# Scatters and gathers ordered by pick in a sparse expert layer: tiles wait for the level of their expert, gathers for the last expert of their pick

## The reference

```python
logits = jnp.einsum('bsh,eh->bse', x, router_w) + expert_bias
scores = jax.nn.softmax(logits, axis=-1)
top_w, top_idx = jax.lax.top_k(scores, TOP_K)          # TOP_K = 4
top_w = top_w / jnp.sum(top_w, axis=-1, keepdims=True)
g = jnp.einsum('bsh,khe->bske', x, gate_proj)          # 16 x (256, 224)
u = jnp.einsum('bsh,khe->bske', x, up_proj)
act = jax.nn.silu(g) * u
out = jnp.einsum('bske,keh->bskh', act, down_proj)     # 16 x (224, 256)
sel = jnp.take_along_axis(out, top_idx[..., None], axis=2)
return jnp.sum(sel * top_w[..., None], axis=2)
```

## Time and profile before

| | us |
|---|---|
| median of three runs (lowest, highest) | 670.77 (670.66, 671.4) |
| the profiled execution | 671.04 |
| its span in the trace | 669.1 |
| first scatter issued | 106.14 |
| first expert tile's load issued | 149.01 |
| first gather issued, last gather issued | 262.28, 301.69 |
| PE busy in the span | 545.4 (82%) |

### The profile page before, as it was taken

One profiled execution on the slowest core, in us unless ns is written; L12 is line 12 of the kernel. 1 busy time (PEld: TensorE's weight loads), 2 busy tenths in 40 slices (PEclk: granted clock), 3 DMA queues, 4 the chain that ended last, 5 costly groups with the idle time before them and its releaser, 6 DMA issues.

```text
span 669.1 us, 10928 instructions
## 1 busy us (share of the span) xinstructions
PE 545.4 (82%) x3365; PEld 470.0 (70%) x3365; DVE 372.1 (56%) x989; ACT 228.5 (34%) x583; POOL 267.5 (40%) x247
## 2 busy tenths in 40 slices
PE   7898966009999999305987796699999999999994
PEld 4665655008998988203653374599999999999994
DVE  4665685703444444563999865866444444444445
ACT  4653432203555554213501033123333233323334
POOL 4473025751678962770378600310431404314000
PEclk9996897557999999655999877789999999999998
DMA  8999301622667764430000030020202102000001
GB/s 251 383 387 382 122 1 64 219 93 73 200 194 227 215 207 131 142 106 21 0 1 0 18 124 1 0 72 1 72 1 72 42 30 71 0 0 0 0 0 63
DMA packets 54571, 66.71 MB, mean 100 GB/s; under 512 B 5745, under 2 KB 49538, under 8 KB 54530
## 3 DMA queue, kind: packets, MB, share of 16 engines
q10 hardware_dynamic: 31872, 31.07, 13.7%
q1 hardware_dynamic: 19298, 26.18, 12.5%
q0 software_dynamic: 3360, 8.93, 4.3%
HBM read 36.02 MB, written 30.15 MB: 99 GB/s over the span
## 4 chain that ended last, share of the span: by engine, by line
PE 61%; DVE 11%; POOL 9%; issue 5%; DMA 4%; ACT 2%; ACTq 0%; POOLq 0%; DVEq 0%
PE PS L1646 45%; POOL FA L671 4%; POOL xg L636 4%; PE PS L1914 3%; DMA FA<-xg 3%; DVE FA L1600 2%; DVE PS L1582 2%; PE PS L1939 1%; PE PS L1743 1%; PE PS L1721 1%; PE PS L2034 1%; PE PS L1963 1%; PE PS L2046 1%; PE PS L1706 1%; DVE EQ L1369 1%
## 5 line engine op out<-in xcount | busy, mean ns | idle before, releaser
L1646 PE MATMUL PS<-EW,XH 128*128 128x384 f32 (+2 forms) x732 | 208.7, 367 | 6.0 <-DVE SQ L1398 4.4
L1646 PEld LDWEIGHTS PS<-EW,XH 128*128 128x128 f32 x732 | 126.5, 193 | 10.5 <-DVE SQ L1398 4.7
L1398 DVE SCALAR_TENSOR_TENSOR SQ<-SIL,CW,PS 128x96 f32<-128x96 f32 x256 | 69.1, 311 | 115.7 <-ACT SIL L846 114.8
L1646 PE MATMUL PS<-EW,XL 128*128 128x384 f32 (+2 forms) x366 | 129.4, 353 | 0.0
L1646 PE MATMUL PS<-EW,EHH 128*128 128x256 f32 (+1 forms) x476 | 101.8, 289 | 0.2
L846 ACT ACTIVATE SIL<-PS 128x192 f32<-128x192 f32 x128 | 42.5, 332 | 160.8 <-PE PS L1646 160.8
L1646 PE MATMUL PS<-EW,EHL 128*128 128x256 f32 (+1 forms) x286 | 80.2, 281 | 0.0
L1646 PEld LDWEIGHTS PS<-EW,EHH 128*128 128x128 f32 (+1 forms) x476 | 78.0, 188 | 1.2 <-issue 0.5
L602 POOL TENSOR_TENSOR round_mark<-round_mark 128x1 f32<-128x1 f32 x10 | 2.2, 217 | 181.0 <-PE PS L1646 132.0
L1646 PEld LDWEIGHTS PS<-EW,XL 128*128 128x128 f32 x366 | 70.2, 192 | 2.1
L1646 PEld LDWEIGHTS PS<-EW,EHL 128*128 128x128 f32 (+1 forms) x286 | 53.8, 188 | 0.0
(11 more groups left out here) (348 smaller groups left out, 1058.0 us busy)
## 6 DMA issues: line engine op xcount, KB each, us to landing
xg<-EQ ACTq DMA_DIRECT2D x1, 16384.0 KB, 61.5
EG<-in_gateup SPq DMA_DIRECT2D x16, 448.0 KB, 4.1
FA<-xg ACTq DMA_DIRECT2D x47, 128.0 KB, 2.5
yg<-FA ACTq DMA_DIRECT2D x47, 128.0 KB, 2.2
ED<-in_down SPq DMA_DIRECT2D x16, 224.0 KB, 4.5
EG<-in_gateup SPq DMA_DIRECT2D x4, 768.0 KB, 4.6
FA<-in_gateup SPq DMA_DIRECT2D x4, 768.0 KB, 4.7
yg<-EQ ACTq DMA_DIRECT2D x1, 1920.0 KB, 8.6
```

What stands on the lines that cost most here:

```text
L1398: ins = dve.scalar_tensor_tensor(out=HH[:, pos % 2, h:h + W], in0=SIL[:, s, j * W:(j + 1) * W], scalar=c, in1=bank(s)[:, I + j * W:I + (j ...
L1646: ins = pe.matmul(o, l, r, start=start and i == 0, stop=stop and i == n - 1, skip_group_check=True)
```

## The change

1. The picks of a token are sorted by expert number, smallest first: DVE negates the four indices and takes MAX8 of them per token tile. So pick 0 can be of experts 0 to 12, pick 1 of 1 to 13, pick 2 of 2 to 14, pick 3 of 3 to 15. The softmax over the picks is now taken over all 16 logits, and the picks' weights are selected from that inside the tile loop.
2. The scatters go by pick. First 14 of the first half's 16 (picks 0 to 2, then pick 3 of tiles 0 and 1), then the second half's by pick, with the first half's last two among them. When all eight of a pick have landed POOL raises `level` by one (`landed`).
3. A tile's load waits for the level of its expert (expert 0: level 1; 1: 2; 2: 3; others: 4), read from a table for each of the first 12 tiles. Before, the first load waited for all 32 scatters.
4. The gathers go by pick. All tiles' pick 0 when the stores up to pick 0's last expert have landed, then pick 1 likewise, then picks 2 and 3 by tile when all are stored. PE adds 8 small matmuls that count the picks by expert (`picked_experts`), for the last expert of each pick. With this case's inputs these are experts 10, 12 and 15, so 30, 34 and 40 tiles. The marks are made three times. An eighth `BACK` buffer lies in `OGATE`.
5. `pack_slots`, the weights and the store counts are cut in seven parts that DVE does inside the tile loop, after iterations 8, 10, 12 (weights), 14, 16, 18 (rows) and 20 (counts).
6. All 47 tiles of `yg` are zeroed, and that transfer moves forward into the first attention (unit 28 of its 40).

```diff
+            for k in range(TOP0 - 1):
+                for t in range(HALF):
+                    scatter(t, k)
+            for t in range(HALF // 2):
+                scatter(t, TOP0 - 1)
+            pool.wait_ge(slots_ready, 2)
+            pool.wait_ge(x_act, NT)
+            for k in range(TOP0 - 1):
+                for t in range(HALF, NT):
+                    scatter(t, k)
+                    if k > 0 and t == HALF + 1:
+                        landed(k - 1)
+            for t in range(HALF // 2, NT):
+                scatter(t, TOP0 - 1)
+                if t == HALF // 2 + 1:
+                    landed(TOP0 - 2)
+            landed(TOP0 - 1)
+            pool.wait_ge(level, TOP0)
...
+            for k in range(2):
+                stored_up_to(k, k)
+                for t in range(NT):
+                    gather(t, k)
+            stored_up_to(TOP0 - 1, 2)
             for t in range(NT):
...
+                for k in range(2, TOP0):
+                    gather(t, k)
...
+                if u == YG_ZERO_AT:
+                    act.dma_start(yg.rearrange("(n p) d -> p n d", p=P),
...
+                if i < EARLY_TILES:
+                    act.wait_ge(level, act.value_load(tile_level[0:1, i:i + 1], min_val=1, max_val=TOP0))
+                elif i == EARLY_TILES:
+                    act.wait_ge(level, TOP0)
...
-                act.wait_ge(scattered, 16 * NT * TOP0)
...
+                ch.link(dve.tensor_scalar(t1[:, tiles, 0:TOP0], tix[:, tiles, 0:TOP0], -1.0, None, ALU.mult))
+                for t in half_tiles(f):
+                    ins = dve.max(tif[:, t, :], t1[:, t, :])
+                ch.link(ins)
...
+                    if i in WEIGH_AT:
+                        pick_weights(WEIGH_AT.index(i))
+                    if i in PACK_AT:
+                        pack_slots(PACK_AT.index(i))
+                    if i == STORES_AT:
+                        store_counts()
```

More of the change, by code:

```diff
@@ L159, in build_kernel @@
         row_f = FA[0:1, 1920:1920 + TABLE]
-        fours = FA[0:1, 1984:1985]
+        fours = FA[0:1, 1872:1872 + TOP0]
+        reached = FA[0:1, 1984:1984 + E0 * TOP0]
         XG = FA[:, 2048:3072].rearrange("p (s d) -> p s d", s=4)
@@ L356, in build_kernel @@
         tables_ready = sem("tables_ready")
-        scattered = sem("scattered")
+        scattered = [sem(f"scattered{k}") for k in range(TOP0)]
+        level = sem("level")
+        picked_mm = sem("picked_mm")
         xg_ld = [sem(f"xg_ld{i}") for i in range(4)]
@@ L629, in _, with scatter, landed @@
             pool.wait_ge(xg_zero, 16)
[L630 to L638, removed]
+            def scatter(t, k):
+                n = t * TOP0 + k
+                pool.indirect_dma_start(
+                    out=xg, out_offset=bass.IndirectOffsetOnAxis(ap=slots[:, n:n + 1], axis=0),
+                    in_=XB[:, t, :], in_offset=None).then_inc(scattered[k], 16)
+            def landed(k):
+                pool.wait_ge(scattered[k], 16 * NT)
+                if k > 0:
+                    pool.wait_ge(level, k)
+                pool.tensor_tensor(round_mark[:, 0:1], round_mark[:, 1:2], round_mark[:, 2:3], ALU.add).then_inc(level, 1)
+            pool.wait_ge(slots_ready, 1)
+            pool.wait_ge(x_act, HALF)
+            for k in range(TOP0 - 1):
[16 more added lines that the diff above has]
+            pool.wait_ge(level, TOP0)
             pool.wait_ge(tables_ready, 1)
@@ L947, in _ @@
             act.wait_ge(rt_max, 1)
-            act.activation(t3[:, :, 0:TOP0], t1[:, :, 0:TOP0], ACT.Exp).then_inc(rt_exp, 1)
+            act.activation(LG[:, :, E0:2 * E0], LG[:, :, E0:2 * E0], ACT.Exp).then_inc(rt_exp, 1)
             warm(ACT.Silu)
@@ L1452, in pack_slots, with store_counts @@
+            def store_counts():
                 big = float(1 << 23)
-                ch.link(dve.tensor_scalar(fours, last, 1.6, 0.25, ALU.add, ALU.mult))
+                ch.link(dve.tensor_reduce(fours, reached.rearrange("p (e k) -> p k e", e=E0), AX_X, ALU.max))
+                ch.link(dve.tensor_scalar(fours, fours, 1.6, 0.25, ALU.add, ALU.mult))
                 ch.link(dve.tensor_scalar(fours, fours, big, None, ALU.add))
                 ch.link(dve.tensor_scalar(fours, fours, -big, 16.0, ALU.add, ALU.mult))
-                dve.tensor_copy(stores_to[:, 0:1], fours)
@@ L1812, in ranks, with picked_experts @@
                           stop=True, skip_group_check=True).then_inc(rank_mm, 1)
+            def picked_experts():
+                pe.wait_ge(x_act, HALF)
+                for t in range(NT):
+                    ins = pe.matmul(bank(4)[:, 0:E0 * TOP0], onesb, picks[:, t].rearrange("p e k -> p (e k)"),
+                                    start=(t == 0), stop=(t == NT - 1), skip_group_check=True)
+                ins.then_inc(picked_mm, 1)
             def heads_to_tokens(b):
```

104 lines of the change are left out of this document (63 added, 41 removed).

## The result

The changed kernel takes 642.94 us (median of 4 runs, 642.42 to 643.75), the kernel before 670.71 beside it. The ratio is 0.961, 95% interval 0.955 to 0.967: faster. The profiled execution took 643.75 (span 641.9).

The account below looks back on a forecast made before the run. Bound: mostly TensorE's matmuls, with gathers and scatters 4% each. Start 16.5 us, less 0.5 in the loop, plus 16.2 of filled wait, less marks, less 5.2 for DVE: 21.2 us earlier, 649.5 us; own range 646 to 654, wider 644 to 657.

Parts of the forecast that it names:

- Part 1: From scatters to first tile load: load at 132.5 instead of 149.01, 16.5 us earlier, with no waits for later levels.
- Part 2: Seven DVE parts inside the tile loop: 0.5 us delay for all together, ends 0 and 5.6.
- Part 3: POOL after its splits: gathers fill a 16.2 us wait, less three sets of marks of 1.9 each.
- Part 4: Combining of token tiles: DVE becomes the bound, 23.0 us from tile 0 to tile 7, giving 5.2 back.
- Rival (b): Combining keeps pace with the gathers, so tile 7 starts 26.4 us earlier, 644.3 us; chance 9%.
- Part 5: Zeroing of yg in the first attention: 22.6 us of transfer, over before the first tile load, costing 0.
- (a): Levels or POOL's own waits eat part of the early start: marks wait for landed transfers, 6 us, 655.5; chance 10%.
- (c): First tile load comes no earlier, its level in effect reached only with all scatters: 4.0 us gain, 666.8; chance 7%.
- (d): Slower: sixteen gathers beside tile loads and stores each wait for the one before, 45 us longer, 694.5; chance 4%.

Follow-up runs that it names:

- e8: Changed kernel with each of its first eight gathers waiting until one more expert tile, from tile 38 on, is done; 654.87 us, ratio 0.985 to the kernel before.
- after: The profiled execution of the unedited changed kernel in its first measurement; 643.75 us, span 641.9.
- e2: Changed kernel with gathers by pick, but all tiles wait for level 4; 694.21 us, ratio 1.002 to the kernel before.
- before: The profiled execution of the kernel before, from which the prediction worked; 671.04 us, span 669.1.
- c0: The kernel before, unedited, run once more in the third group of experiments; 668.17 us.
- e6: Changed kernel with the seven DVE parts ahead of the tile loop and twelve of the 32 adds inside its last eight iterations; 644.56 us, ratio 0.968.
- e9: Changed kernel whose 32 gathers fetch 64 bytes a token instead of 1024, from other rows; 641.78 us, ratio 0.964 to the kernel before.
- e3: Kernel before with only the change's two small DVE operations added in dispatch_constants, results unused; 693.29 us, ratio 1.001 to the kernel before.
- c1: The changed kernel, unedited, run once more in the second group of experiments; 686.13 us, ratio 0.991 to the kernel before.
- the first two groups: Two of three sets of experiments with edited and unedited kernels; the kernel before took 695.07 and 692.23 us beside them, 667.31 in the third.

## Why the prediction was right, and where it was off

**What bounds, and the early start (Part 1): right.** Forecast from first scatter to first load 132.5 - 106.59 = 25.9, measured 26.21. The marks cost less than supposed (mark and next scatter 0.36 instead of 0.5), level 4 came 44.1 behind the first scatter (forecast 43.5), and tile 4 loaded at 137.47, 3.7 behind its level (forecast 2.3). One load, tile 8's at 146.90, fell next to level 4's mark at 146.88, but in e8 it went at 144.91, ahead of that mark at 145.34, so it waits for level 3 only, and I count no wait for a level. The reason was right, and in undisturbed executions the start reaches the first output whole.

**Parts in the loop (Part 2): size off, cause open in part.** From first load to the end of the last split 97.1 before and 99.1 after, where 0.5 was forecast. In after, a part that met POOL's split took longer:

```profile
154.97 2.28 DVE L1508 TENSOR_TENSOR FA<-PR,LG 128x512 f32<-128x512 bf16 x1
```

```profile
154.58 2.12 POOL L688 TENSOR_TENSOR EW<-EG,EW 128x896 fp32r<-128x896 f32 x1
156.65 0.65 POOL L690 TENSOR_TENSOR round_mark<-round_mark 128x1 f32<-128x1 f32 x1
```

The product takes 0.68 to 0.74 in the other seven profiles that have it in the loop, and a TENSOR_SCALAR on 1x4 beside a split (186.31) took 1.26 instead of 0.16. Right behind each of the two, PE stands idle ahead of a gate-and-up product. The profile names no releaser, but by the kernel's order that product waits for the split `XL`, which DVE does only after its part (157.28 and 187.49):

```profile
157.96 0.67 PE L1734 MATMUL PS<-EW,XH 128*128 x2 [0.53 <-issue]
```

```profile
188.16 0.67 PE L1734 MATMUL PS<-EW,XH 128*128 x2 [0.85 <-issue]
```

That is 1.4 us instead of 0.5, and it is the prediction's own sign of being wrong in this part, a gap of PE of over half a microsecond in tiles 8 to 20. In e8 the second is there alone (0.89), in e2 too (1.35); before, c0 and e6, without parts in the loop, have none of the kind. Yet e6's stretch is 99.2 all the same: its first output comes 0.9 later, and PE waits 1.6 us in it for tile loads (after 0.9, before 1.5). So the parts cost some 1 us, but moving them won nothing. What remains is within what executions differ by: with the change's loop the stretch is 97.5 in e8 and 97.6 in e9, without it 97.1 in before, 96.0 in c0 and 98.0 in e3. Its cause stays open.

**POOL (Part 3): right, marks mis-sized.** The last split ended at 228.1 (forecast 230.1); counted from the first scatter, which came 3.8 earlier, that is 1.8 later than forecast. A set of marks with its register loads took 1.3 us and not 1.9; the three gave 1.9 back. The last gather went out at 270.88, forecast 275.3. No set waited for a store. Between the last split and the first gather lay 16.2 us before and 1.3 after, and e8 shows that POOL's time there reaches tile 7 nearly whole (10.4 of 10.7).

**Combining (Part 4): right.** 22.66 us from tile 0 to tile 7, forecast 23.0. Rival (b), a combine that keeps the gathers' pace, is refuted: DVE waited 1.6 us for gathers in two places (11.2 before), and where no gather stands beside it at all (c1, 298.47 to 320.64) it takes 22.2.

**Zeroing (Part 5): right.** Issued at 74.87, landed 20.6 us later, 33 us ahead of the first load.

**The sum.** In the profiled execution 643.75 against 649.8: 6.05 less. 3.8 are the first attention's (first scatter 102.76 instead of 106.59), 1.2 the tail behind tile 7, 1.0 the changed stages (marks -1.9, combining -0.3, loop +1.5, small waits -0.3), so that two errors, marks and loop, nearly cancel. The step that failed is the one left out: that all ahead of the first scatter stays as it was but for 0.45. The prediction has no term for TensorE's clock there, nor for the two operations of DVE that the change puts into the first attention. In the profiles TensorE falls to its lower level at 32, at 48 or at 55 us, or not up to 75, and the first scatter lies anywhere from 101.1 to 106.8. The two operations go with a part of this, but the five falls ahead of them and c0 (104.25 where before has 106.14) show that chance has a part too; how much of the 3.8 is the change's own stays open. The median of 642.94 lies nearer to rival (b)'s 644.3 than to the forecast, but by the first attention and not by (b)'s mechanism. (The upper terms of the prediction's own range add up to 6.3, so to 655.8 and not 654; the miss was on the lower side.) Of the rivals, (a) and (c) did not occur. (d) had the wrong mechanism: the gathers kept 1.27 us even where everything else was disturbed. But its outcome, that what stands beside indirect transfers may eat the gain, is what the first two groups showed: tile 7 at 186.6 instead of 149.5 behind the first load. The kernel before paid there too (178.9 instead of 155.5, e3), so the change still won, by 0.9% (c1).

## What to carry to other kernels

Where an engine waits for a batch of stores or scatters as a whole and has a row of issues of its own to make, sort the work by when its need is met, and price the gain as the wait that is filled, up to the point where another engine's own sum takes over (22 us of adds here). Spreading DVE's adds into a stretch in which POOL issues transfers gains nothing when POOL's issue is next on the path. A sum that reaches over a long stretch of matmuls should carry a term for the granted clock, even where the change hardly touches the stretch: two executions of the kernel before ended it 1.9 us apart, the fourteen profiles 5.7.

## What the runs showed of the hardware

- The same kernel took 643 and 686 us, and before 667 and 695 on one chip in two groups of runs. Between the profiles of after and c1, 38 of the 43 us lay beside rows of POOL's indirect transfers, also in engines that don't touch them; c1's row of 3.61 us between two DVE operations shows it best. Its cause was not found.
- DVE and POOL ran slower beside each other, in both directions: four marks 1.76 instead of 1.02 and a gather's issue 1.84 instead of 0.95 beside two DVE adds each (the next gather kept 0.95), a DVE product 2.28 instead of 0.69 beside a POOL split. The Trainium skill says in "SBUF — State Buffer", section "Who interferes with whom", that these two engines share a port pair under an exclusive lock, and that a DVE instruction with two SBUF inputs contends with a GpSimd instruction that reads SBUF. By that rule the adds, which read two tiles, would hold up the marks, and the trace of e6 agrees; so does the product in after. Gathers beside the combining behind the loop, which has the same adds, kept 1.288 us against 1.27, so for the issue of gathers no run shows a rule: one of them lost 0.9.
- An indirect gather of 128 rows costs POOL 1.27 us, of 64 bytes a row or of 1 KB.
